# Transposing 24 token blocks by 32x32 squares and device memory instead of on TensorE, tiles through device memory too, and a later GpSimd split

## The chip, the core and the metric

The kernel runs on one core of a Trainium2 chip. The metric is the device time of one execution in microseconds (us): 2503.42 us before, the median of 3 runs from 2503.2 to 2503.71. Engines are named by the profile's letters: PE is TensorE's matmul, PEld its weight load, DVE is VectorE, ACT ScalarE, POOL GpSimd, SP SyncE. ACTq is ScalarE's own queue, where it issues its transfers.

## What is computed

One transformer layer between two half-weighted feed-forward blocks, on 4 x 1024 tokens of 512 values, all in float32:

```python
def ffn(x, W1, W2, W3):                       # W1, W3 (2048, 512), W2 (512, 2048)
    hidden = silu(x @ W1.T) * (x @ W3.T)
    return fwht(hidden) @ W2.T                # Walsh-Hadamard transform over the 2048
def attn(x, wq, wk, wv, wo, inv_freq):
    q, k = rope(heads(x @ wq.T)), rope(heads(x @ wk.T)); v = heads(x @ wv.T)   # 16 heads of 32
    weights = softmax(einsum("bshd,bstd->bsht", q, k) / sqrt(32))   # heads of one token among themselves
    return einsum("bsht,bstd->bshd", weights, v).reshape(b, s, 512) @ wo.T
x = x + 0.5 * ffn(layernorm(x), W1, W2, W3)
x = x + attn(layernorm(x), wq, wk, wv, wo, inv_freq)
x = x + 0.5 * ffn(layernorm(x), W1, W2, W3)
```

The scores are taken between the 16 heads of each token, so attention needs nothing from other tokens.

## The kernel before

The 4096 tokens are 8 tiles of 512, and a tile is 4 blocks ("subs", numbered 0 to 31) of 128 tokens. There are 16 passes, numbered 0 to 15: each of the 8 tiles runs through the feed-forward twice, and `PASSES` holds the order, `(1, t)` for a tile's first time and `(2, t)` for its second. The Walsh-Hadamard transform is folded into W2 during pass 0. Every float32 matrix product is made of three fp32r matmuls, with both operands split into a high and a low part (L608 to L610, `products`; for the down projection also L639, L640 and L643).

**A pass.** `feed_forward(p)` has 16 steps n of 128 hidden values. In a step TensorE makes the gate and the up half, 2 x 4 x 3 = 24 matmuls of 512 columns from the tile's transposed input `xt` (`up`), and then adds the hidden slice of the step before to the 4 banks of `acc`, 4 x 3 = 12 matmuls (`down`). ScalarE applies SiLU (L1076), VectorE multiplies by the up half (L1584), ScalarE copies the product to fp32r (L1084, the high part), VectorE subtracts (L1591, the low part). TensorE needs both parts of step n-1 only after it has made up(n). At the end of a pass there is no next up step: down(14) follows up(15) at once, and down(15) waits for L1591 of step 15.

**Attention** is done by VectorE between these steps, for blocks whose q, k and v are ready. It is cut in 512 units, 16 a block, each a product and a reduction of 128 x 1024 (L1311 and L1323 for scores, L1316 and L1325 for values). `UNITS_TO` says how many units a pass does, and `units_by_step` deals them out over its steps, against planned costs: 2.5 for a unit, and a cost of its own for each piece of other VectorE work (`beside`) in a step. ScalarE's exponential of a block stands ahead of or behind its hidden copy of a step (`EXP_AHEAD`, `EXP_BEHIND`), which follows from where the units stand.

**Gaps.** Between two passes TensorE makes q, k and v of two or three new blocks (`new_subs(p)`), 12 matmuls for each of q, k and v of a block, and in some passes the output projection of a tile. Passes 5, 14 and 15 (`LATE`) take a tile through attention's output projection right before its second feed-forward: their gap is `late_gap`, all others' is `early_gap`. A block is "early" when its tile was finished a pass ahead; 24 of the 32 are. `rope(g)` rotates q and k of block g on VectorE (four products L1281 from PSUM, four sums L1293 and L1294 from SBUF), and TensorE's first up step of a pass waits for the rotation of the second new block (`s_rope`), as it needs its PSUM banks.

**Who transposes what.** A matmul needs the token axis across columns, so a normalised block must be transposed. For an early block VectorE normalises it in step 13 (`Q_APPLY`, L1225) into `prod[:, 2]`; TensorE transposes it with four 128 x 128 matmuls against the identity (`transpose_sub`, L689), which stand between up(15) and down(14) of the pass ahead of an `early_gap`, and inside a `late_gap`; ScalarE and VectorE split the result from PSUM to `sub_xt` (L935, L1189). The tile of the next pass, where that is not `LATE` (11 passes, `MOVED`), goes another way: VectorE normalises it in steps 8 and 9 and transposes it within 32 x 32 squares (L1562), 16 transfers of 64 KB from SBUF to SBUF (`move`, L945, four in each of steps 10 to 13) put the squares in place, ScalarE copies the high part in step 14 (L952), and VectorE subtracts in step 15 (L1568). Finished attention outputs of five tiles go through device memory in squares as well (`keep_output` L957, `move_outputs` L966).

**The first gap.** After pass 0 GpSimd still splits the four raw attention weights (L1164). The last four of these splits, for the output projection, run beside `rope(0)`. ScalarE may write the values of the first blocks only when they are done (`s_wattn` 4).

**Weights.** SyncE loads 1 MB of up weights (L573) and 512 KB of down weights (L576) for every step from device memory, two buffers each.

## Time and profile before

| | |
|---|---|
| median of 3 runs | 2503.42 us |
| the profiled execution | 2501.66 us |
| its span | 2499.8 us, granted clock 1.0 |
| PE busy | 2489.7 us, 100% of the span, 11111 instructions |
| DVE busy | 2044.3 us, 82%, 2602 |
| ACT busy | 530.2 us, 21%, 796 |
| POOL busy | 63.0 us, 3%, 109 |
| DMA | 459.48 MB; SyncE's queue 46.0% and ScalarE's 5.7% of the 16 engines |
| device memory | 408.04 MB read, 38.80 MB written |

The chain of work that ended last is 90% PE and 8% DVE. The share of a busy engine counts from the start of its first to the end of its last overlapping instruction: a matmul of 512 columns is listed with 0.39 us, but they follow each other every 0.227 us. In a timeline row stand the start, the duration, engine, line, operation, written and read tiles with their shapes, the count of merged instructions, and in brackets the idle time before it and what ended it.

### The profile page before, as it was taken

Reading aid. Unit: us, or ns where it says so; the run is one execution under the profiler, and the core shown is the slowest. Engines: PE = TensorE matmul, PEld = TensorE weight load, DVE = VectorE, ACT = ScalarE, POOL = GpSimd, SP = SyncE. Lnnn points to the kernel's source line nnn. Section 1 sums busy time; section 2 is a strip of 40 time slices with the busy share of each in tenths; the row PEclk is TensorE's granted clock in tenths of the full one; section 3 lists DMA queues with packets and bytes.
Section 4 is the critical chain, followed back from the end, with each engine's and each line's share of the span. In section 5 each row is a group of like instructions: output and inputs, shape, how many; then the busy total and the mean of one; then the engine's idle time right before and its main releaser. Section 6 shows DMA issues by size and latency. Waiting matters only on the chain.

```text
span 2499.8 us, 30169 instructions
## 1 busy us (share of the span) xinstructions
PE 2489.7 (100%) x11111; PEld 2061.4 (82%) x11111; DVE 2044.3 (82%) x2602; ACT 530.2 (21%) x796; POOL 63.0 (3%) x109
## 2 busy tenths in 40 slices
PE   9999999999999999999999999999999999999999
PEld 7878888888888888888888888888888888888887
DVE  9569989699786997979969899797986979878711
ACT  3332212222121221222212122122121212211211
POOL 0030000000000000000000000000000000000000
PEclk9999999999999999999999999999999999999999
DMA  9645635455352564645635466454562545535364
GB/s 343 254 188 181 218 145 200 131 202 210 135 201 81 210 216 162 224 131 206 207 109 188 168 229 208 146 220 144 202 221 93 197 148 219 190 107 199 137 219 165
DMA packets 161172, 459.48 MB, mean 184 GB/s; under 512 B 53312, under 2 KB 82240, under 8 KB 127808
## 3 DMA queue, kind: packets, MB, share of 16 engines
q1 hardware_dynamic: 81792, 419.73, 46.0%
q10 hardware_dynamic: 79296, 38.68, 5.7%
q8 instruction: 46, 0.75, 0.1%
q14 instruction: 38, 0.31, 0.0%
HBM read 408.04 MB, written 38.80 MB: 179 GB/s over the span
## 4 chain that ended last, share of the span: by engine, by line
PE 90%; DVE 8%; issue 1%; DMA 0%; ACT 0%; POOL 0%; SPq 0%; DVEq 0%; ACTq 0%; POOLq 0%
PE gu L608 19%; PE gu L610 19%; PE gu L609 19%; PE acc L639 8%; PE acc L640 8%; PE acc L643 8%; PE acc L608 2%; PE acc L610 2%; PE acc L609 2%; DVE scores L1323 1%; DVE mixed L1325 1%; DVE prod L1316 1%; DVE prod L1311 1%; PE acc L736 1%; DVE gated L1584 1%
## 5 line engine op out<-in xcount | busy, mean ns | idle before, releaser
L608 PE MATMUL gu<-xt,w_up 128*128 128x512 f32 x2048 | 798.4, 390 | 0.2
L610 PE MATMUL gu<-xt,w_up 128*128 128x512 f32 x2048 | 796.8, 389 | 0.0
L609 PE MATMUL gu<-xt,w_up 128*128 128x512 f32 x2048 | 796.7, 389 | 0.0
L608 PEld LDWEIGHTS gu<-xt,w_up 128*128 128x128 f32 x2048 | 384.4, 188 | 80.7 <-issue 0.8
L609 PEld LDWEIGHTS gu<-xt,w_up 128*128 128x128 f32 x2048 | 384.4, 188 | 80.0
L610 PEld LDWEIGHTS gu<-xt,w_up 128*128 128x128 f32 x2048 | 384.4, 188 | 79.8
L1584 DVE TENSOR_TENSOR gated<-gated,gu 128x512 f32<-128x512 f32 x240 | 162.8, 679 | 239.8 <-PE gu L610 238.3
L639 PE MATMUL acc<-w_down,hid 128*128 128x512 f32 x896 | 349.6, 390 | 0.0
L640 PE MATMUL acc<-w_down,hid 128*128 128x512 f32 x896 | 348.6, 389 | 0.0
L1084 ACT ACTIVATE hid<-gated 128x512 fp32r<-128x512 f32 x240 | 152.0, 633 | 892.2 <-DVE gated L1584 882.6
L1325 DVE TENSOR_REDUCE mixed<-prod 128x64 f32<-128x1024 f32 x256 | 310.1, 1213 | 0.0
L1311 DVE TENSOR_TENSOR prod<-tok 128x1024 f32<-128x1024 f32 x256 | 309.1, 1219 | 1.0
L1323 DVE TENSOR_REDUCE scores<-prod 128x32 f32<-128x1024 f32 x256 | 309.6, 1213 | 0.0
L1316 DVE TENSOR_TENSOR prod<-scores,tok 128x1024 f32<-128x1024 f32 x256 | 307.6, 1213 | 1.2
L1076 ACT ACTIVATE gated<-gu 128x512 f32<-128x512 f32 x240 | 143.7, 599 | 591.5 <-PE gu L610 588.5
L643 PE MATMUL acc<-w_down,hid 128*128 128x512 f32 x896 | 239.5, 389 | 0.0
L643 PEld LDWEIGHTS acc<-w_down,hid 128*128 128x128 f32 x896 | 168.2, 188 | 35.0
L640 PEld LDWEIGHTS acc<-w_down,hid 128*128 128x128 f32 x896 | 168.2, 188 | 34.6
L639 PEld LDWEIGHTS acc<-w_down,hid 128*128 128x128 f32 x896 | 168.2, 188 | 34.6
L1591 DVE TENSOR_TENSOR hid<-gated,hid 128x512 fp32r<-128x512 f32 x240 | 163.8, 682 | 20.2 <-ACT hid L1084 20.2
L608 PE MATMUL gu<-w_attn,sub_xt 128*128 128x512 f32 x232 | 90.7, 391 | 0.0
L609 PE MATMUL gu<-w_attn,sub_xt 128*128 128x512 f32 x232 | 90.3, 389 | 0.0
(144 smaller groups left out, 1946.8 us busy)
## 6 DMA issues: line engine op xcount, KB each, us to landing
w_up<-up_pairs SPq DMA_DIRECT2D x240, 1024.0 KB, 4.9
w_down<-down_pairs SPq DMA_DIRECT2D x240, 512.0 KB, 3.5
up_pairs<-w_up SPq DMA_DIRECT2D x16, 1024.0 KB, 5.1
xt<-tok ACTq DMA_DIRECT2D x176, 64.0 KB, 4.1
prod<-up_raw SPq DMA_DIRECT2D x16, 512.0 KB, 6.3
down_pairs<-w_attn SPq DMA_DIRECT2D x4, 2048.0 KB, 18.4
out<-x ACTq DMA_DIRECT2D x7, 1024.0 KB, 5.3
x<-x ACTq DMA_DIRECT2D x6, 1024.0 KB, 6.5
```

The lines of the kernel that those rows point to most:

```text
L608: nc.tensor.matmul(o, w_hi, m_hi, start=first, stop=False)
L609: nc.tensor.matmul(o, w_hi, m_lo, start=False, stop=False)
L610: return nc.tensor.matmul(o, w_lo, m_hi, start=False, stop=last)
L639: nc.tensor.matmul(acc[:, s, :], h_hi[:, s * P:(s + 1) * P], hi, start=first, stop=False)
L640: nc.tensor.matmul(acc[:, s, :], h_hi[:, s * P:(s + 1) * P], lo, start=False, stop=False)
L643: ins = nc.tensor.matmul(acc[:, s, :], h_lo[:, s * P:(s + 1) * P], hi, start=False, stop=False)
L1311: return nc.vector.tensor_tensor(prod[:, buf, :].rearrange("p (h t d) -> p h t d", h=2, t=HEADS), wide(q[:, h:h + 2, None, :], 2, HEADS), ...
L1316: return nc.vector.tensor_tensor(prod[:, buf, :].rearrange("p (h d t) -> p h d t", h=2, d=HD), wide(scores[:, g % 2, h:h + 2, None, :], 2, ...
L1323: return nc.vector.tensor_reduce(scores[:, g % 2, h:h + 2, :], prod[:, buf, :].rearrange("p (h t d) -> p h t d", h=2, t=HEADS), AX.X, ALU.add)
L1325: return nc.vector.tensor_reduce(mixed[:, h:h + 2, :], prod[:, buf, :].rearrange("p (h d t) -> p h d t", h=2, d=HD), AX.X, ALU.add)
L1584: nc.vector.tensor_tensor(by_token(gated[:, u, :]), by_token(gated[:, u, :]), from_bank(gu[:, 2 * u + 1, :], p), ALU.mult).then_inc(s_h, 1)
L1591: nc.vector.tensor_tensor(low, gated[:, u, :], high.bitcast(FP32), ALU.subtract).then_inc(s_hid_lo, 1)
```

## The change

Five things are changed.

1. **Early blocks.** TensorE no longer transposes the 24 early blocks (`MOVED_SUBS`). VectorE normalises them in step 11 instead of 13 and transposes each in place within 32 x 32 squares. ScalarE stores each to device memory in step 12 (`keep_sub_squares`, 256 KB), reads it back in place in four transfers of 64 KB with pieces of 128 bytes (`move_sub`, the first block in step 13, the second in step 14), and copies the high part in step 15 (`moved_sub_high`, for all early blocks). VectorE subtracts (`moved_sub_low`). The eight blocks that are not early (0, 1, 2, 4, 11, 18, 24, 27) keep TensorE's transpose.
2. **Tiles.** A tile's squares no longer go from SBUF to SBUF. One transfer of 1 MB stores them in step 10 (`keep_squares`), four of 256 KB with pieces of 512 bytes read them back in step 11 (`move`), and the high copy stands in step 13 instead of 14.
3. **ScalarE's order.** In a step the stores and reads now come ahead of the exponentials that stand behind the hidden copy.
4. **The gap's order.** Where the second new block isn't early (blocks 4 and 24, ahead of passes 2 and 11), its transpose moves from between q and k of the first block to behind them, and v of the first block now comes before q and k of the second.
5. **GpSimd.** The last four weight splits wait for `rope(0)`.

The planner's cost of step `Q_APPLY` becomes 1.25 a block, which deals the units out a little differently: in pass 5 from `3 3 2 3 3 3 2 2 2 2 2 3 3 2 3 0` to `3 3 3 2 3 3 2 3 1 2 3 1 3 3 3 0`.

```diff
-X_STATS, X_APPLY, X_MOVE, X_SPLIT, Q_STATS, Q_APPLY = 6, 8, 10, 14, 10, 13
+X_STATS, X_APPLY, X_KEEP, X_MOVE, X_SPLIT = 6, 8, 10, 11, 13
+Q_STATS, Q_APPLY, Q_KEEP, Q_MOVE, Q_SPLIT = 10, 11, 12, 13, 15
+MOVED_SUBS = {g: at for at, g in enumerate(g for p in range(2, NP) for g in early_subs(p))}
-    beside[Q_APPLY] += 0.55 * len(early_subs(p + 1))
+    beside[Q_APPLY] += 1.25 * len(early_subs(p + 1))
+        tile_squares = nc.dram_tensor("tile_squares", [P, SUBS * D], FP32).ap()
+        sub_squares = nc.dram_tensor("sub_squares", [2, P, D], FP32).ap()
...
# TensorE
-            def query_key(g, between=None):
-                split_ready("q", g, 0)
+            def query_key(g):
+                if g in MOVED_SUBS:
+                    pe.wait_ge(s_sub_lo, MOVED_SUBS[g] + 1)
+                else:
+                    split_ready("q", g, 0)
...
             def late_gap(p):
-                output(p, 0)
-                output(p, 1)
-                if new:
-                    pe.wait_ge(s_added, SUBS * p)
-                    transpose_sub(new[0])
-                    transpose_sub(new[1])
-                output(p, 2)
-                output(p, 3)
+                for s in range(SUBS):
+                    output(p, s)
                 if new:
                     pe.wait_ge(s_x2, SUBS * i + 2)
                     query_key(new[0])
-                    split_ready("q", new[1], 0)
...
                 pe.wait_ge(s_h, HT * p)
+                query_key(new[0])
+                pe.wait_ge(s_added, SUBS * p)
                 if is_early(p, 1):
-                    query_key(new[0])
+                    query_key(new[1])
+                    value(new[0])
                 else:
-                    query_key(new[0], lambda: transpose_sub(new[1]))
-                pe.wait_ge(s_added, SUBS * p)
-                query_key(new[1])
-                value(new[0])
+                    transpose_sub(new[1])
+                    value(new[0])
+                    query_key(new[1])
...
                 else:
-                    pe.wait_ge(s_h, n0 + HT - 1)
-                    for g in early_subs(after):
-                        transpose_sub(g)
                     down_step(last, 0, False, False)
                 down_step(last, 1, False, True)
...
# ScalarE
-            def move(p, q):
-
+            def keep_squares(p):
                 act.wait_ge(s_turned, SUBS * MOVED[p] + SUBS)
-                squares = turned.rearrange("p (k f c) -> p k f c", k=KT, f=QUADS)
+                act.dma_start(tile_squares, turned).then_inc(s_squares_kept, 16)
+
+            def move(p):
+
+                act.wait_ge(s_squares_kept, 16 * MOVED[p] + 16)
+                squares = tile_squares.rearrange("(q i) (k f c) -> f i k q c", q=QUADS, k=KT, f=QUADS)
...
+            def keep_sub_squares(g):
+                act.wait_ge(s_sub_turned, MOVED_SUBS[g] + 1)
+                act.dma_start(sub_squares[new_subs(next_of(g)).index(g)], sub_normed(g)).then_inc(s_sub_kept, 16)
+
+            def move_sub(g):
+
+                later = max(early_subs(next_of(g)))
+                act.wait_ge(s_sub_kept, 16 * MOVED_SUBS[later] + 16)
+                squares = sub_squares[new_subs(next_of(g)).index(g)].rearrange("(q i) (k f j) -> f i k q j", q=QUADS, k=KT, f=QUADS)
+                for f in range(QUADS):
+                    act.dma_start(sub_split(g)[1][32 * f:32 * f + 32].bitcast(FP32).rearrange("p k (q j) -> p k q j", q=QUADS),
+                                  squares[f]).then_inc(s_sub_moved, 16)
+
+            def moved_sub_high(g):
+                later = max(early_subs(next_of(g)))
+                act.wait_ge(s_sub_moved, 16 * QUADS * (MOVED_SUBS[later] + 1))
+                high, low = sub_split(g)
+                nc.scalar.activation(high, low.bitcast(FP32), ACT.Copy).then_inc(s_sub_hi, 1)
...
                     nc.scalar.activation(hidden(u)[0], gated[:, u, :], ACT.Copy).then_inc(s_hid_hi, 1)
-                    if n == HT - 1 and after < NP and after not in LATE:
+                    for g in OUTPUT_KEEP.get((p, n), ()):
+                        keep_output(g)
+                    if after in MOVED and n == X_KEEP:
+                        keep_squares(after)
+                    if after in MOVED and n == X_MOVE:
+                        move(after)
+                    if after < NP and n == Q_KEEP:
                         for g in early_subs(after):
-                            sub_high(g)
+                            keep_sub_squares(g)
+                    if after < NP and Q_MOVE <= n < Q_MOVE + len(early_subs(after)):
+                        move_sub(early_subs(after)[n - Q_MOVE])
                     for g in EXP_BEHIND.get((p, n), ()):
                         exp(g)
-                    for g in OUTPUT_KEEP.get((p, n), ()):
-                        keep_output(g)
-                    if after in MOVED and X_MOVE <= n < X_MOVE + QUADS:
-                        move(after, n - X_MOVE)
                     if after in MOVED and n == X_SPLIT:
                         moved_high(after)
+                    if after < NP and n == Q_SPLIT:
+                        for g in early_subs(after):
+                            moved_sub_high(g)
...
# GpSimd
                 for k in range(KT):
+                    if m == O and k == 0:
+                        pool.wait_ge(s_rope, 1)
...
# VectorE
+            def moved_sub_low(g):
+                dve.wait_ge(s_sub_hi, MOVED_SUBS[g] + 1)
+                high, low = sub_split(g)
+                nc.vector.tensor_tensor(low, low.bitcast(FP32), high.bitcast(FP32), ALU.subtract).then_inc(s_sub_lo, 1)
...
                             for s, g in enumerate(early):
                                 ln_apply(key, s, sub_normed(g), x_of(g))
+                            for s, g in enumerate(early):
+                                dve.wait_ge(s_ln, ln_done(key, s))
+                                squares = sub_normed(g).rearrange("p (f j) -> p f j", j=32)
+                                nc.vector.transpose(squares, squares).then_inc(s_sub_turned, 1)
```

The order of instructions shows it at four places. First TensorE at the end of pass 3, between up(15) (`gu<-xt,w_up`) and down(14) (`acc<-w_down,hid`), before:

```order
L609 MATMUL gu<-xt,w_up 128x512
L610 MATMUL gu<-xt,w_up 128x512
L689 MATMUL gu<-ident,prod 128x128 x8
L639 MATMUL acc<-w_down,hid 128x512
L640 MATMUL acc<-w_down,hid 128x512
```

and now:

```order
L619 MATMUL gu<-xt,w_up 128x512
L620 MATMUL gu<-xt,w_up 128x512
L649 MATMUL acc<-w_down,hid 128x512
L650 MATMUL acc<-w_down,hid 128x512
L649 MATMUL acc<-w_down,hid 128x512
```

The eight transposes are gone, and the down step follows the up step directly.

TensorE in the gap ahead of pass 2, before, where q of block 3 ends, block 4 is transposed and k of block 3 begins:

```order
L609 MATMUL gu<-w_attn,sub_xt 128x512
L610 MATMUL gu<-w_attn,sub_xt 128x512
L689 MATMUL gu<-ident,prod 128x128 x4
L608 MATMUL gu<-w_attn,sub_xt 128x512
L609 MATMUL gu<-w_attn,sub_xt 128x512
```

and now, where k of block 3 ends, block 4 is transposed and v of block 3 begins:

```order
L619 MATMUL gu<-w_attn,sub_xt 128x512
L620 MATMUL gu<-w_attn,sub_xt 128x512
L699 MATMUL gu<-ident,prod 128x128 x4
L618 MATMUL acc<-w_attn,sub_xt 128x512
L619 MATMUL acc<-w_attn,sub_xt 128x512
```

q and k of block 4 (24 matmuls) used to stand ahead of v of blocks 3 and 4, and stand now between the two.

ScalarE from the hidden copy of step 13 of pass 5 on (the next pass has blocks 12 and 13 early), before (the gate's SiLU is `gated<-gu`, the hidden copy `hid<-gated`):

```order
L1084 ACTIVATE hid<-gated 128x512
L945 DMA xt<-tok 32x4x128 x4
L1076 ACTIVATE gated<-gu 128x512
L1084 ACTIVATE hid<-gated 128x512
L957 DMA out_squares<-tok 128x512
L952 ACTIVATE xt<-xt 128x1024 x2
L1076 ACTIVATE gated<-gu 128x512
L1084 ACTIVATE hid<-gated 128x512
L935 ACTIVATE sub_xt<-gu 128x512 x2
```

and now:

```order
L1113 ACTIVATE hid<-gated 128x512
L974 DMA sub_xt<-sub_squares 32x16x32 x4
L959 ACTIVATE xt<-xt 128x1024 x2
L1105 ACTIVATE gated<-gu 128x512
L1113 ACTIVATE hid<-gated 128x512
L986 DMA out_squares<-tok 128x512
L974 DMA sub_xt<-sub_squares 32x16x32 x4
L1105 ACTIVATE gated<-gu 128x512
L1113 ACTIVATE hid<-gated 128x512
L981 ACTIVATE sub_xt<-sub_xt 128x512 x2
```

The four transfers of block 12 are followed by the tile's copy in step 13, those of block 13 stand in step 14, and the blocks' copies of step 15 read `sub_xt` where the transfers have put it, not PSUM.

VectorE in pass 5, around the normalising of blocks 12 and 13, before in step 13:

```order
L1311 TENSOR_TENSOR prod<-tok 128x1024
L1323 TENSOR_REDUCE scores<-prod 128x32
L1225 TENSOR_SCALAR prod<-x,mean_var,rstd 128x512 x2
L1584 TENSOR_TENSOR gated<-gated,gu 128x512
L1311 TENSOR_TENSOR prod<-tok 128x1024
```

and now in step 11:

```order
L1357 TENSOR_TENSOR prod<-scores,tok 128x1024
L1366 TENSOR_REDUCE mixed<-prod 128x64
L1638 TENSOR_TENSOR hid<-gated,hid 128x512
L1266 TENSOR_SCALAR prod<-x,mean_var,rstd 128x512 x2
L1625 STREAM_TRANSPOSE prod<-prod 128x512 x2
L1631 TENSOR_TENSOR gated<-gated,gu 128x512
L1357 TENSOR_TENSOR prod<-scores,tok 128x1024
```

Two transposes of 128 x 512 stand behind the two normalisations, and the next step's product waits behind them.

## Rows read from the trace of the kernel before

**Rows 1.** The page's busy times by engine: us, share, instructions.
```profile
PE 2489.7 (100%) x11111; PEld 2061.4 (82%) x11111; DVE 2044.3 (82%) x2602; ACT 530.2 (21%) x796; POOL 63.0 (3%) x109
```

**Rows 2.** TensorE's waits over the span: total us, times, longest.
```profile
PE gu L608 <- DVE tok L1294: 2.2, 1, 2.2
...
PE acc L608 <- DVE hid L1591: 0.8, 2, 0.4
PE gu L689 <- DVE prod L1225: 0.6, 2, 0.4
```

**Rows 3.** TensorE's timeline at the end of pass 2: start, us, instruction.
```profile
460.46 0.40 PE L610 MATMUL gu<-xt,w_up 128*128 128x512 f32 x1
460.70 1.04 PE L689 MATMUL gu<-ident,prod 128*128 128x128 f32 x8
...
461.81 0.40 PE L640 MATMUL acc<-w_down,hid 128*128 128x512 f32 x1
```

**Rows 4.** TensorE's timeline at the end of pass 1.
```profile
312.16 0.39 PE L610 MATMUL gu<-xt,w_up 128*128 128x512 f32 x1
312.40 0.60 PE L689 MATMUL gu<-ident,prod 128*128 128x128 f32 x4
...
313.06 0.40 PE L640 MATMUL acc<-w_down,hid 128*128 128x512 f32 x1
```

**Rows 5.** VectorE's timeline at the end of pass 1, step 15.
```profile
312.66 0.69 DVE L1584 TENSOR_TENSOR gated<-gated,gu 128x512 f32<-128x512 f32 x1
314.05 0.69 DVE L1591 TENSOR_TENSOR hid<-gated,hid 128x512 fp32r<-128x512 f32 x1 [0.70 <-ACT hid L1084]
```

**Rows 6.** Window: us, busy us (xcount) of PE, PEld, DVE, ACT, POOL; passes 3, 5, 6, 8, 9.
```profile
500.60:620.00 119.40, 119.40 (x528) 98.86 (x527) 116.10 (x136) 26.35 (x38) 2.10 (x4) 1.00 0.57 207
...
819.40:938.80 119.40, 119.40 (x528) 98.82 (x527) 118.78 (x140) 26.35 (x38) 2.10 (x4) 1.00 0.63 227
967.20:1086.60 119.40, 119.40 (x529) 98.80 (x528) 118.68 (x143) 29.09 (x41) 2.10 (x4) 1.00 0.63 225
...
1293.80:1413.20 119.40, 119.40 (x528) 98.84 (x527) 118.77 (x140) 26.36 (x38) 2.10 (x4) 1.00 0.58 209
1441.60:1561.00 119.40, 119.40 (x528) 98.81 (x527) 117.84 (x142) 29.22 (x41) 2.10 (x4) 1.00 0.64 228
```

**Rows 7.** Timelines at the end of passes 5 and 6, TensorE.
```profile
938.81 1.03 PE L689 MATMUL gu<-ident,prod 128*128 128x128 f32 x8
...
1086.58 1.03 PE L689 MATMUL gu<-ident,prod 128*128 128x128 f32 x8
```

**Rows 8.** Timelines at the end of passes 5 and 6, VectorE.
```profile
939.30 0.68 DVE L1584 TENSOR_TENSOR gated<-gated,gu 128x512 f32<-128x512 f32 x1
...
1088.54 0.68 DVE L1584 TENSOR_TENSOR gated<-gated,gu 128x512 f32<-128x512 f32 x1
```

**Rows 9.** VectorE's timeline in step 8 of pass 5.
```profile
890.48 1.30 DVE L1562 STREAM_TRANSPOSE tok<-prod 128x512 f32<-128x512 f32 x2
891.70 0.65 DVE L1584 TENSOR_TENSOR gated<-gated,gu 128x512 f32<-128x512 f32 x1
```

**Rows 10.** VectorE's timeline in the gap ahead of pass 2, rotating block 4.
```profile
330.33 0.69 DVE L1281 TENSOR_TENSOR prod<-gu,cos_t 128x512 f32<-128x512 f32 x1 [1.49 <-PE gu L610]
...
333.96 0.42 DVE L1294 TENSOR_TENSOR tok<-prod 128x256 f32<-128x256 f32 x1
```

**Rows 11.** The first gap: GpSimd's timeline.
```profile
165.68 5.38 POOL L1164 TENSOR_TENSOR w_attn<-tok,w_attn 128x512 fp32r<-128x512 f32 x4 [2.08 <-ACT w_attn L1043]
```

**Rows 12.** The first gap: VectorE's timeline.
```profile
168.44 1.50 DVE L1294 TENSOR_TENSOR tok<-prod 128x256 f32<-128x256 f32 x1
169.86 1.48 DVE L1293 TENSOR_TENSOR tok<-prod 128x256 f32<-128x256 f32 x1
```

**Rows 13.** ScalarE's transfer issues of L945: ns min/median/max.
```profile
L945 ACTq DMA_DIRECT2D xt<-tok x176: 592/622/1395, 272.6 to 2023.2; - x176
```

**Rows 14.** ScalarE's transfer issues of L966: ns min/median/max.
```profile
L966 ACTq DMA_DIRECT2D xt<-out_squares x20: 578/1650/4993, 463.5 to 1876.2; - x20
```

More of the change, by code:

```diff
@@ L173, in transposed @@
         elif p in LATE:
-            order += att + [("q", g, 0) for g in new[:2]] + [("x", p, k) for k in range(KT)]
+            order += att + [("x", p, k) for k in range(KT)]
         else:
-            order += [("q", g, 0) for g in early_subs(p)]
             order += [("q", g, 0) for j, g in enumerate(new[:2]) if not is_early(p, j)] + att
@@ L359, in build @@
         s_turned = sem("s_turned")
+        s_squares_kept = sem("s_squares_kept")
         s_moved = sem("s_moved")
@@ L362, in build @@
         s_moved_lo = sem("s_moved_lo")
+        s_sub_turned = sem("s_sub_turned")
+        s_sub_kept = sem("s_sub_kept")
+        s_sub_moved = sem("s_sub_moved")
+        s_sub_hi = sem("s_sub_hi")
+        s_sub_lo = sem("s_sub_lo")
         s_att_turned = sem("s_att_turned")
@@ L696, in project @@
                 return ins
-            def query_key(g, between=None):
-                split_ready("q", g, 0)
+            def query_key(g):
[3 more added lines that the diff above has]
+                    split_ready("q", g, 0)
                 project(Q, qk_bank(g)[:, Q, :], sub_split(g), 0)
-                if between is not None:
-                    between()
                 project(K, qk_bank(g)[:, K, :], sub_split(g), 0).then_inc(s_qk, 1)
@@ L952, in moved_high, with next_of @@
                     nc.scalar.activation(X[:, 0, ks, :], X[:, 1, ks, :].bitcast(FP32), ACT.Copy).then_inc(s_moved_hi, 1)
+            def next_of(g):
+                return next(p for p in range(2, NP) if g in new_subs(p))
+            def keep_sub_squares(g):
[13 more added lines that the diff above has]
+                nc.scalar.activation(high, low.bitcast(FP32), ACT.Copy).then_inc(s_sub_hi, 1)
             def keep_output(g):
@@ L1113, in gap @@
                     attention_high(p)
-                    for g in new[:2]:
-                        sub_high(g)
                     for k in range(KT):
@@ L1576, in beside @@
                         if n == Q_APPLY:
+                            if after in MOVED:
+                                dve.wait_ge(s_turned, SUBS * MOVED[after] + SUBS)
                             for s, g in enumerate(early):
                                 ln_apply(key, s, sub_normed(g), x_of(g))
+                            for s, g in enumerate(early):
+                                dve.wait_ge(s_ln, ln_done(key, s))
+                                squares = sub_normed(g).rearrange("p (f j) -> p f j", j=32)
+                                nc.vector.transpose(squares, squares).then_inc(s_sub_turned, 1)
                 for n in range(HT):
@@ L1594, in feed_forward @@
                         for g in early:
-                            sub_low(g)
+                            moved_sub_low(g)
                     beside(n)
@@ L1615, in late_gap @@
                         for g in new[:2]:
-                            sub_low(g)
+                            moved_sub_low(g)
                 ln_means(key, at, last_of(key))
@@ L1668, in early_gap @@
                         dve.wait_ge(s_added, SUBS * (p - 1) + 1)
-                    else:
-                        dve.wait_ge(s_tp, TP["q", new[0], 0] + 1)
                     sub_stats(just[0])
```

6 lines of the change are left out of this document (3 added, 3 removed).

## The prediction

> **What bounds the kernel now.** I read the page's busy times first. TensorE is busy for 2489.7 us of a span of 2499.8, VectorE for 2044.3 [rows 1]. So nearly every microsecond taken from TensorE's stream counts, unless a wait takes its place. TensorE's waits come next: the list adds up to some 8 us, and three entries matter here: 2.2 us once behind a rotation of VectorE (L1294), 0.8 us in two waits of 0.4 at a pass's end behind the hidden low part (L1591), and 0.6 us in two waits of a transpose [rows 2]. Third, busy time by pass, because VectorE's 82% is a mean. In passes 5, 6 and 8 VectorE is busy for 118.7 to 118.8 of 119.4 us, so between two products there is no idle time; pass 9 has 0.9 us less work, and pass 3 has 2.7 us less [rows 6]. The same rows give TensorE's pitch, 119.4 us for 528 listed matmuls or 0.227 us each, so that 12 matmuls take 2.72 us and 24 take 5.44. The timelines of TensorE and VectorE at a pass's end come last, since there down(14) is the only cover for the hidden split of step 15.
>
> **TensorE's transposes.** At the end of pass 2 eight of them stand between the matmuls that start at 460.46 and 461.81. That is 1.35 us, of which two pitches (0.45) would be there anyway: 0.90 us for two blocks [rows 3]. Four of them at the end of pass 1 give 0.90 - 0.45 = 0.45 us for one block [rows 4]. The listed durations (1.04 and 0.60) overlap their neighbours and aren't used. 24 blocks x 0.447 us = **10.7 us less**. 20 of the blocks stand at pass ends and four in the two late gaps, where the output projections follow each other and VectorE follows them with the same distance as before, so I count those whole.
>
> **What is late next at a pass's end.** Without transposes TensorE arrives at down(15) 2.72 us after up(15). In pass 1 up(15) ends at 312.40 [rows 4], the product starts at 312.66, and the low part ends at 314.05 + 0.69 = 314.74 [rows 5]: 2.34 us, or 0.26 us to the product's start and 2.08 from there. That fits under 2.72 with 0.4 us to spare, so in a pass whose VectorE is on time the transposes' time is won in full. But each pass gets VectorE work. One more transpose pair: the pair L1562 starts at 890.48 and the next product at 891.70, so **1.22 us** for two blocks [rows 9]. It comes in step 11, and where there is idle time behind it, it costs nothing. Passes 5, 6 and 8 have none [rows 6]:
> - Pass 5: the last product starts 939.30 - 938.81 = 0.49 us after up(15) [rows 7, 8]. Then 0.49 + 1.22 + 2.08 = 3.79, against 2.72: a wait of 1.1 us. Pass 8 has the same busy time [rows 6], so another 1.1.
> - Pass 6: 1088.54 - 1086.58 = 1.96 [rows 7, 8]. Then 5.26 against 2.72, 2.5 us, of which one of the 0.4 us waits was there [rows 2]: 2.1 more.
> - Pass 9: its 0.9 us less busy time takes up most of the pair; about 0.3.
>
> Together **4.6 us more**. The ends of this term are 0 (the planner, whose cost for the step rises, finds room that the rows don't show) and about 9 (each of the other eight passes also gets half a microsecond, for the units come out in other steps and VectorE's lateness in a step reaches 5 us or more). I take the value by rows, since a VectorE without a gap can't hide anything. The other wait of 0.4 us, in pass 2, I leave as it is: ScalarE's tile copy moves from before the last SiLU, but VectorE's last reduction ends late there too.
>
> **The gaps ahead of passes 2 and 11.** Block 4 (and 24) is projected later: behind its q and k only v of one block stands, 2.72 us, where there were two, 5.44. The first up step needs the rotation's end. It starts about 0.2 us after the matmuls and runs from 330.33 to 333.96 + 0.42 = 334.38, so 4.05 us [rows 10]. 0.2 + 4.05 - 2.72 = 1.5 us of waiting, twice: **3.1 us more**. The bounds are 0 and 4.5 (block 3's rotation also starts later, behind the split of block 4). The transpose itself comes 2.7 us later than now and no longer waits for its normalised input: **0.6 us less** [rows 2].
>
> **The first gap.** Beside GpSimd's four splits (165.68 to 171.06) [rows 11] two sums of `rope(0)` take 1.50 and 1.48 us [rows 12], where the same instruction takes 0.42 with GpSimd idle [rows 10]. With the splits behind the rotation these 2.1 us go, and TensorE's wait of 2.2 us [rows 2] with them: **2.1 us less**. What is behind the wait: the rotation then ends at about 169.6 and the splits at 175.0; ScalarE writes its first value block after TensorE's next 24 matmuls, 16 transposes and 12 matmuls (5.4 + 1.8 + 2.7 us), at about 179.5, so nothing is held up. `rope(1)` meets the last split and may lose one microsecond; TensorE has the tile's transposes in front of it there.
>
> **Transfers and ScalarE.** A pass with a tile issued 16 transfers over four steps; now it issues 1, 4, 2, 4 and 4 in steps 10 to 14. One L945 issue takes 0.62 us [rows 13], so four take 2.5 us, as a step's four do today. From the hidden copy to the next SiLU ScalarE has 4.4 us (a step of 8.16 minus 1.0 and 2.72), and VectorE needs that SiLU only 2.7 us later. But L966's issues (2048 pieces each) take from 0.58 to 4.99 us, 1.65 in the median [rows 14]; 0.6 + 5.0 + 2 x 1.65 makes 8.9 us for four. The new transfers have 512 pieces each. So a step's issues cost between 2.5 and 8.9 us; I take 2.5 to 4.5, since 2048 pieces in all are what a single L966 has, and hidden either way. Stores land a step ahead of the reads that wait for them, and the reads of step 14 have 8 us until the copy of step 15. I cost all of this at nothing.
>
> The Trainium skill speaks against this part: DMA: Bandwidth & Descriptors (Specifications) puts the least size for full rate at 512 B, and has smaller pieces read and modified, so the blocks' 128-byte pieces would be the slow kind. In this trace the only 128-byte reads are L966's, and they are the slow ones. By the rule alone the sum would move to the fourth rival below; by the count of pieces it stays.
>
> **Sum.** -10.7 + 4.6 + 3.1 - 0.6 - 2.1 = -5.7 us. The profiled execution took 2501.66 us, which makes 2496.0 for it; it lies 1.8 us under the median of the runs, so the median goes from 2503.42 to **2497.7 us**.
>
> **Rivals.**
> 1. *VectorE's extra work is absorbed.* For it: 18% of VectorE is idle over the span, and the planner now knows the cost. Against it: passes 5, 6 and 8 are full by the rows. Then -10.7 + 3.1 - 0.6 - 2.1 = -10.3: 2493.1 us.
> 2. *VectorE's lateness spreads.* Half a microsecond at the ends of the other eight passes: 2501.7 us. For it: only 0.4 us of cover is left anywhere. Against it: those passes had 1 us and more of idle time.
> 3. *The removed time was filler everywhere*, because the splits of the blocks (which now wait for a transfer) come late: TensorE needs them 5.4 us after up(15), and they are ready at about 4. It would give no change, 2503 us.
> 4. *Slower: ScalarE's issues block.* If the four small-piece reads of step 14 take 8.9 us as L966's can, they begin 1.0 us after up(14) and end 1.7 us after up(15). The last SiLU (0.6) then ends at 2.3, and product, copy and subtraction (2.1) at 4.4: a wait of 1.7 us in nine passes and about 3 us more in the three full ones, 24 us in all. 2497.7 + 24 = 2522 us. It decides from issues of 6 us on, which is where the SiLU comes later than up(15). Short of that it gives nothing.
>
> **Numbers.** Forecast 0.50, rival 1 0.20, rival 2 0.15, rival 3 0.05, rival 4 0.07, and 0.03 for what I don't see. What a measurement can tell from no change is 0.2%, 5.0 us, so the border is 2498.4 us, right beside my number. The forecast's own range is 2494.5 to 2500.5, and I give it 0.29 faster and 0.21 same. With rival 1 that makes 0.49 faster; the forecast's 0.21 with rivals 2 and 3 makes 0.41 the same; rival 4 and the unseen make 0.10 slower. The range 2491 to 2505 takes in rivals 1 to 3 and leaves out the fourth.
>
> **What would show it.** No transpose row at the ends of passes 2 to 13, and 96 transposes fewer. TensorE's waits behind the hidden low part: 1.1 us in passes 5 and 8, 2.5 in pass 6. A wait of 1.5 us of the first up step behind the rotation in passes 2 and 11. No wait in the first gap, and sums of 0.42 us there. ScalarE's issues of `sub_xt` at 0.6 us each; a single one of over 3 us would point to rival 4. The forecast is wrong if VectorE's last product starts no later than now in pass 5, or if TensorE waits inside a pass.

## The result, and the profile after

The changed kernel takes **2515.12 us** (median of 8 runs, 2509.21 to 2522.78), against 2503.39 us for the kernel before on the same chip: a ratio of 1.0049 [1.0039, 1.0059], slower by 12 us where I forecast 6 us less. The profiled execution is the slowest of the eight, 2522.78 us with a span of 2521.0; so its waits are those of the worst of the eight, and their sum is more than the median lost. The page's busy times, to be held against [rows 1]:

```profile
PE 2488.4 (99%) x11015; PEld 2055.8 (82%) x11015; DVE 2058.8 (82%) x2626; ACT 531.1 (21%) x796; POOL 63.5 (3%) x109
```

The 96 transposes are gone (11111 to 11015), and VectorE has 14.5 us more. TensorE's waits, whose counterparts are [rows 2] (line, waited for, total us, times, longest):

```profile
PE gu L618 <- DVE sub_xt L1247: 14.6, 4, 5.1
PE acc L618 <- DVE hid L1638: 8.0, 7, 3.2
PE gu L618 <- DVE tok L1335: 4.1, 3, 1.4
```

The first line is new: four times TensorE waits for the low part of a block's input. The single waits from TensorE's timeline, in the gaps ahead of passes 1 and 2 and at the ends of passes 5, 6, 8 and 11 (a wait for `sub_xt` is that of the first product of the gap behind):

```profile
178.06 0.47 PE L618 MATMUL gu<-w_attn,xt 128*128 128x512 f32 x1 [1.20 <-DVE tok L1335]
335.27 0.50 PE L618 MATMUL gu<-xt,w_up 128*128 128x512 f32 x1 [1.43 <-DVE tok L1335]
...
941.52 0.47 PE L618 MATMUL acc<-w_down,hid 128*128 128x512 f32 x1 [2.42 <-DVE hid L1638]
948.26 0.77 PE L618 MATMUL gu<-w_attn,sub_xt 128*128 128x512 f32 x1 [3.74 <-DVE sub_xt L1247]
1098.26 0.47 PE L618 MATMUL acc<-w_down,hid 128*128 128x512 f32 x1 [3.20 <-DVE hid L1638]
1102.56 0.47 PE L618 MATMUL gu<-w_attn,sub_xt 128*128 128x512 f32 x1 [1.32 <-DVE sub_xt L1247]
1425.44 0.47 PE L618 MATMUL acc<-w_down,hid 128*128 128x512 f32 x1 [1.13 <-DVE hid L1638]
1432.87 0.77 PE L618 MATMUL gu<-w_attn,sub_xt 128*128 128x512 f32 x1 [4.43 <-DVE sub_xt L1247]
1895.99 0.77 PE L618 MATMUL gu<-w_attn,sub_xt 128*128 128x512 f32 x1 [5.13 <-DVE sub_xt L1247]
```

Read the end of pass 5 on ScalarE and VectorE. The reads of the second block (L974) are issued at 932.27, behind an output's store:

```profile
931.90 0.33 ACTq L986 DMA_DIRECT2D out_squares<-tok  x1
932.27 6.30 ACTq L974 DMA_DIRECT2D sub_xt<-sub_squares  x4
938.67 0.60 ACT L1105 ACTIVATE gated<-gu 128x512 f32<-128x512 f32 x1 [6.14 <-issue]
939.30 0.69 DVE L1631 TENSOR_TENSOR gated<-gated,gu 128x512 f32<-128x512 f32 x1 [1.18 <-ACT gated L1105]
940.02 0.63 ACT L1113 ACTIVATE hid<-gated 128x512 fp32r<-128x512 f32 x1 [0.75 <-DVE gated L1631]
946.76 1.15 ACT L981 ACTIVATE sub_xt<-sub_xt 128x512 fp32r<-128x512 f32 x2 [6.12 <-DMA sub_xt<-sub_squares]
```

The same four issues by themselves (ns of one, least, median and longest, with the first and last start; then us from an issue to its landing):

```profile
L974 ACTq DMA_DIRECT2D sub_xt<-sub_squares x4: 564/772/4101, 932.3 to 937.9; - x4
DMA to landing us min/median/max: 6.4/9.2/9.7
```

Two things went wrong. The four issues took 6.30 us instead of 2.6, one of them 4.10 us by itself, so the SiLU behind them started at 938.67 and VectorE's last product waited 1.18 us for it. And ScalarE's copy, ready after 940.65, waited 6.12 us for the data, which landed 14 us after the first issue; VectorE's subtraction and TensorE's q follow it. The window view of these microseconds (us, busy us of the engines, then granted clock, DMA share, GB/s) shows the DMA engines full while TensorE waits (SyncE's loads of the up and down weights are issued at 931.8 and 931.0, and again at 936.7 and 939.3), and TensorE's clock at half behind the wait:

```profile
936.00:941.00 5.00, 3.10 (x14) 2.25 (x12) 3.13 (x4) 1.23 (x2) 0.00 (x0) 1.00 1.02 324
941.00:947.00 6.00, 3.00 (x12) 2.17 (x12) 0.37 (x1) 0.24 (x1) 0.00 (x0) 0.96 0.61 165
948.00:950.00 2.00, 1.74 (x4) 1.48 (x5) 2.00 (x4) 0.00 (x0) 0.00 (x0) 0.50 0.00 0
950.00:952.00 2.00, 2.00 (x6) 1.52 (x6) 2.00 (x3) 0.00 (x0) 0.00 (x0) 0.50 0.00 0
952.00:954.00 2.00, 2.00 (x8) 1.58 (x7) 1.38 (x3) 0.00 (x0) 0.00 (x0) 0.66 0.00 0
```

The four passes have one thing in common: where the second block's reads fall against SyncE's up loads. In passes 5, 8 and 11 they are issued 0.50, 0.48 and 0.33 us behind one and in pass 6 2.18 us behind one, and the four issues take 6.30, 3.72, 4.28 and 3.21 us. In the other seven passes that read a second block they come 1.1 to 2.7 us ahead of an up load and take 2.6 to 2.8 us, as in pass 3:

```profile
613.55 2.80 ACTq L974 DMA_DIRECT2D sub_xt<-sub_squares  x4
614.61 5.23 SPq L583 DMA_DIRECT2D w_up<-up_pairs  x2
```

Back at the end of pass 5, from 948.26 on twelve matmuls take until 953.44, 5.2 us instead of 2.7. Behind the wait of 4.43 us twelve take 5.2 us too, and behind that of 5.13 us seven take 3.0 instead of 1.6: 6.4 us for the three places. The account of the span: it grew by 21.2 us, which is -10.7 for the transposes, +23.1 of waits (26.7 in the three lines above, 3.6 in [rows 2]) and 8.8 left. The clock's 6.4 is the part of them that rows show; 2.4 us stay open.

### The profile page after: what moved, and what is told of

Same layout as the page of the kernel before. It is cut to its first block, busy times and chain, and to the rows that moved or that the text cites. A ratio compares the mean times of both kernels' runs of the same rounds, so it can differ in the third digit from the quotient of the medians.

```text
span 2521.0 us, 29999 instructions
## 1 busy us (share of the span) xinstructions
PE 2488.4 (99%) x11015; PEld 2055.8 (82%) x11015; DVE 2058.8 (82%) x2626; ACT 531.1 (21%) x796; POOL 63.5 (3%) x109
## 4 chain that ended last, share of the span: by engine, by line
PE 72%; DVE 21%; issue 3%; DMA 2%; ACTq 1%; ACT 0%; POOL 0%; DVEq 0%; SPq 0%; POOLq 0%
PE gu L618 16%; PE gu L619 15%; PE gu L620 15%; PE acc L650 6%; PE acc L653 6%; PE acc L649 6%; DVE mixed L1366 4%; DVE scores L1364 4%; DVE prod L1357 3%; DVE prod L1352 3%; PE acc L618 2%; PE acc L620 2%; PE acc L619 2%; DVE gated L1631 2%; DMA sub_xt<-sub_squares 2%
## 5 line engine op out<-in xcount | busy, mean ns | idle before, releaser
L618 PE MATMUL gu<-w_attn,sub_xt 128*128 128x512 f32 x232 | 93.4, 403 | 14.6 <-DVE sub_xt L1247 14.6
L619 PE MATMUL gu<-w_attn,sub_xt 128*128 128x512 f32 x232 | 92.7, 400 | 0.0
```

Source lines behind the costliest of these rows:

```text
L618: nc.tensor.matmul(o, w_hi, m_hi, start=first, stop=False)
L619: nc.tensor.matmul(o, w_hi, m_lo, start=False, stop=False)
```

## The experiments

Every kernel's ratio is against the kernel before on the same chip, whose median was 2501.9 to 2503.4 us in the four sets.

**1. The chain of the blocks one step earlier.**

```diff
-Q_STATS, Q_APPLY, Q_KEEP, Q_MOVE, Q_SPLIT = 10, 11, 12, 13, 15
+Q_STATS, Q_APPLY, Q_KEEP, Q_MOVE, Q_SPLIT = 9, 10, 11, 12, 15
```

> The blocks' statistics, products, stores and reads are each issued one step earlier (steps 9, 10, 11, 12 and 13 in place of 10 to 14); the low part is still made at step 15. Theory A (late landing): the changed kernel lost its time because the second block's four reads, issued in step 14, landed 10.7 to 14.1 us later in passes 5, 6, 8 and 11, and TensorE waited 14.6 us for what is made of them and then ran at half the clock. One step is some 9 us, so the waits for the blocks' low part at the ends of those passes fall from 14.6 us to under 2 and the clock loss of some 9 us goes with them: about 2515 - 13 - 8 = 2494 to 2500. Theory B (VectorE is late by its own work, 1.2 us per transposed pair): its work is the same, so the ends of the full passes wait as before: 2512 to 2518. Theory C (the tiles' transfers and the order of the exponentials cost it): untouched, 2512 to 2518.

Measured: 2533.79 us, 1.0125 [1.0108, 1.0142]. None of the theories. No wait for the blocks' low part is left, so the late landing is cured as theory A had it, but now the blocks' store stands in step 11 behind the tile's reads. ScalarE's timeline in pass 3:

```profile
598.16 4.40 ACTq L952 DMA_DIRECT2D xt<-tile_squares  x4
602.60 2.32 ACTq L966 DMA_DIRECT2D sub_squares<-prod  x2
605.02 0.60 ACT L1105 ACTIVATE gated<-gu 128x512 f32<-128x512 f32 x1 [6.66 <-issue]
606.38 0.63 ACT L1113 ACTIVATE hid<-gated 128x512 fp32r<-128x512 f32 x1 [0.75 <-DVE gated L1631]
613.98 2.64 ACTq L974 DMA_DIRECT2D sub_xt<-sub_squares  x4
616.72 0.60 ACT L1105 ACTIVATE gated<-gu 128x512 f32<-128x512 f32 x1 [9.71 <-issue]
```

The reads wait from 607.0 to 613.98 for the store to land, and the SiLU that is queued behind them and their issues starts after 9.71 us without work on ScalarE. TensorE then waits for the hidden low part, the second line of the changed kernel's list:

```profile
PE acc L618 <- DVE hid L1638: 24.4, 9, 4.2
```

This kernel changed two things at once, the steps and the order against the tile's reads, so it doesn't test the theories' prices. What it shows is that here the reads' wait in front of their issue, which holds up ScalarE's queue, costs more (31 us over the kernel before) than the late landing that it cures (the changed kernel lies 12 us over it).

**2. Exponentials ahead of the transfers within a step.**

```diff
                     nc.scalar.activation(hidden(u)[0], ...).then_inc(s_hid_hi, 1)
+                    for g in EXP_BEHIND.get((p, n), ()):
+                        exp(g)
                     for g in OUTPUT_KEEP.get((p, n), ()):
...
-                    for g in EXP_BEHIND.get((p, n), ()):
-                        exp(g)
```

> Within a step ScalarE issues the exponentials ahead of the stores and reads, as in the kernel before; everything else as in the changed kernel. Theory A (late landing of the block reads in four passes): only pass 11 got its late reads through an exponential that stood behind the tile's reads, so its 5.1 us wait and some 2 us of clock go: about 2507 to 2511. Theory C (the order of exponentials is the cause): the waits go in all four passes, 2495 to 2500. Theory B (VectorE's own work): 2512 to 2518.

Measured: 2519.78 us, 1.0066 [1.0049, 1.0083], which overlaps the changed kernel's interval. The long wait of pass 11 is gone from the trace, as A had it (those of passes 5 and 8 are left, 3.64 and 4.25 us), but a wait of 3.24 us for the hidden low part came in pass 2 and one of 4.27 in pass 6 (3.20 and 1.32, in two waits, in the changed kernel). So the order of the exponentials (theory C) is not the cause, and A's gain of 4 to 8 us did not come: in the trace it was given back in passes 2 and 6, and the time lies above the range of every theory.

**3 and 4. Tiles alone, blocks alone.** The first is the kernel before with the tile's store, reads and split in steps 10, 11 and 13 and GpSimd's wait; the second is the changed kernel with

```diff
-                    if after in MOVED and n == X_MOVE:
-                        move(after)
+                    if after in MOVED and X_MOVE <= n < X_MOVE + QUADS:
+                        move(after, n - X_MOVE)
```

and the old sixteen transfers from `turned` in `move`.

> The kernel before, with the token tiles' squares stored to and read from device memory and GpSimd's last split behind the rotation, and nothing else: the blocks keep TensorE's transposes and the exponentials their place. Theory A (the block reads are the cause): no long wait, within 3 us of the kernel before, 2500 to 2506. Theory C (the tiles' transfers are the cause): most of the loss stays, 2510 to 2520.

> The changed kernel, with the token tiles moved by the sixteen transfers within on-chip memory of the kernel before (steps 10 to 13, copy at step 14). Theory A: the block reads of step 14 stay, so the loss stays: 2511 to 2520, with waits of 3 to 5 us for the blocks' low part at the ends of the full passes. Theory C (the tiles' transfers): 2495 to 2503. If the sixteen transfers' issue on ScalarE costs more than the tile's five, the time is above 2520.

Measured: tiles alone 2500.04 us (2499.73 to 2500.65), 0.9989 [0.9980, 0.9999]; blocks alone 2518.93, 1.0065 [1.0048, 1.0082]. The loss is in the blocks. The first kernel gains 3.1 us by the medians, of which experiment 7 finds 1.0 for GpSimd's wait; its interval nearly reaches no change. In the second kernel the waits are divided otherwise than A said, 14.1 us for the hidden low part and 3.0 for the blocks'. I read the two as one chain on ScalarE, in which a microsecond or two decides which of them catches TensorE; no run tests this.

**5, 6 and 10. The reads in larger pieces, a short transpose, and both.** These lighten the reads and VectorE's work one at a time and then together.

```diff
-                squares = sub_squares[...].rearrange("(q i) (k f j) -> f i k q j", q=QUADS, k=KT, f=QUADS)
+                rows = sub_squares[...].rearrange("p (k c) -> p k c", k=KT)
                 for f in range(QUADS):
-                    act.dma_start(....rearrange("p k (q j) -> p k q j", q=QUADS), squares[f]).then_inc(s_sub_moved, 16)
+                    act.dma_start(..., rows[32 * f:32 * f + 32]).then_inc(s_sub_moved, 16)
```

```diff
-                                squares = sub_normed(g).rearrange("p (f j) -> p f j", j=32)
+                                squares = sub_normed(g)[:, :32].rearrange("p (f j) -> p f j", j=32)
```

> The changed kernel, but each of a block's four reads fetches 32 rows of four 512-byte pieces (512 pieces a block) in place of 2048 pieces of 128 bytes; the same bytes, issues and waits. It leaves out the rearranging of the squares, so the projections get wrong values. Theory A1 (the pieces' number makes the reads land late beside the weights' loads): the reads issue in under 2.7 us and land within 6 us, the waits for the blocks' low part (14.6 us) and the half clock behind them go: 2495 to 2503. Theory B (VectorE comes late by its own added work, whatever the reads cost): 2510 to 2518. Theory A2 (it is the store and the wait for its landing on ScalarE, not the pieces): 2510 to 2518, with the reads' issue short all the same.

> The changed kernel, but VectorE turns only the first 32 of a block's 512 columns (a transpose of some 0.1 us in place of 0.6); it leaves out the rest of the turning, so the projections get wrong values. Stores, reads and order stay. Theory A1 (number of pieces): the loss stays but for VectorE's 1 us a pass: 2507 to 2515. Theory B (VectorE's added 1.2 us a pass makes everything behind it late): the waits of passes 5, 6, 8 and 11 go: 2493 to 2500.

> The changed kernel with both lightenings, 512-byte pieces and a transpose of 32 columns; it leaves out most of the turning, so the projections get wrong values. Theory A (two conditions make the loss: VectorE's added 1.2 us brings the reads beside the weights' loads, and their 2048 pieces make them long there): each alone gave back most, both together give back the rest: 2493 to 2499, with no wait over 2 us but those of the rotation. If they gave back the same microseconds twice and a third cause stays (the short waits for the hidden low part), 2500 to 2504.

Measured: 2505.83 us (2501.65 to 2512.39), 1.0014 [1.0005, 1.0024]; 2502.28 us (2500.51 to 2513.04), 1.0008 [0.9997, 1.0019]; both 2499.18 us (2496.40 to 2505.45), 0.9984 [0.9975, 0.9994]. From the changed kernel's 1.0049 that is 0.35%, 0.41% and 0.65%: 9, 10 and 16 us. Neither A1 nor B alone is right: each edit gives back most of the 12 us, both together more than either and less than the sum of 19. In pass 5 the issue of the four reads, where it took 6.30 us, is in experiments 5 and 6:

```profile
932.77 1.93 ACTq L974 DMA_DIRECT2D sub_xt<-sub_squares  x4
```

```profile
931.77 3.32 ACTq L974 DMA_DIRECT2D sub_xt<-sub_squares  x4
```

The large pieces issue in 1.93 us (over all 96 issues the median of one is 0.44 us instead of 0.66), but ScalarE's copy still waits till 942.98 for them, 10 us after the first issue, where A1 had 6. What the short transpose does can be read from the loads: in passes 5, 8 and 11 the second block's reads now come 0.5 to 0.8 us ahead of the up load instead of 0.3 to 0.5 behind, and the four issues take 3.32, 2.83 and 2.69 us. In all three kernels pass 6 keeps a wait for the hidden low part (3.19, 4.27 and 4.22 us), so that one is not of the reads' length. With both light, one wait of 4.22 us for the hidden low part is left, in pass 6, where an exponential stands behind the first block's reads, and its sum on VectorE waits 2.29 us for it. So the expectation of no wait over 2 us failed, and the time lies between its two ranges.

**7. GpSimd's wait alone.** The kernel before with `pool.wait_ge(s_rope, 1)` ahead of the last split.

> The kernel before with one edit: GpSimd's last split waits for the first rotation. The first gap's wait of 2.2 us goes; in the changed kernel another of 1.2 us stands behind the second rotation, so 1.0 us is won, not the 2.1 that I predicted: 2502.4 (2501.5 to 2503). If the 3.1 us that the tiles' kernel gained are all of this edit, 2500.3.

Measured: 2500.85 us (2500.47 to 2502.26), 0.9993 [0.9984, 1.0002]: 1.0 us in the median, within the interval's reach of nothing. In its trace the rotation's sums take 0.42 us, and the four normalizations of the next tile, beside which the splits now run, take 4.84 us:

```profile
170.81 4.84 DVE L1227 TENSOR_SCALAR tok<-x,mean_var,rstd 128x512 f32<-128x512 f32 x4
```

In the kernel before the same four take 1.91 us there. The cost has moved to them and comes out as 1.2 us of waiting behind `rope(1)`. The median lies below the expected range, but so does that of the kernel before in this set (2501.86 us); the 1.0 us is as expected.

**8. The old order in the gap.** `transpose_sub(new[1])` between the first block's q and k again.

> The changed kernel, with the order of the gap before: the late block's transposes stand between the first block's query and key products. The two waits for the rotation in passes 2 and 11 (1.43 and 1.42 us) go, or become those of the transposes (0.8 us in the kernel before): 2512.5 by the trace (2511 to 2514). If the order mattered for the waits of the low part too, below 2508.

Measured: 2519.1 us (four runs, 2507.65 to 2523.82), 1.0073 [1.0057, 1.0088]. The two rotation waits went (4.1 to 1.2 us) and 1.5 us of transposes' waits came, but the time is undecided: what the edit is worth is far below the spread of 16 us. The profiled execution is its fastest. In pass 5 the reads are issued as in the changed kernel, 0.5 us behind an up load's issue and 1.3 behind a down load's, and yet

```profile
931.84 3.37 ACTq L974 DMA_DIRECT2D sub_xt<-sub_squares  x4
```

and the longest of the four took 6.2 us from issue to landing, against 9.7: the copy could start 7.8 us after the first issue instead of 14.5. The same reads at the same distance from the loads get their data several microseconds sooner or later. In pass 8 of this execution they were slow again, 4.27 us to issue and a wait of 4.67 us of TensorE.

**9 and 12. Which passes carry it.** Two kernels with both routes, on the old gap order: `BY_TENSOR = (6, 7, 9, 12)` leaves the blocks of these four passes to TensorE (16 of 24 by memory), and `BY_TENSOR = (2, 3, 4, 8, 10, 11, 13)` is the counterpart (12 of 24 by memory: the four passes and the late ones).

```diff
+BY_TENSOR = (6, 7, 9, 12)
...
+                    if after in BY_TENSOR:
+                        pe.wait_ge(s_h, n0 + HT - 1)
+                        for g in early_subs(after):
+                            transpose_sub(g)
                     down_step(last, 0, False, False)
```

> The changed kernel with the old gap order, in which the blocks of passes 6, 7, 9 and 12 (8 of 24) are turned by TensorE as in the kernel before and the other 16 by VectorE and device memory. In the changed kernel's trace only the passes ahead of these four lost time behind a late read. Theory A (the loss lies in those four collisions): 16 x 0.447 = 7.2 us of transposes are won, some 1 us more with GpSimd's split, and 1 to 3 us of short waits are lost: 2494 to 2499. Theory D (the collision moves to the passes left, since a pass that is late shifts the weights' loads against the reads anywhere): waits of over 2 us appear in passes 2, 3, 4, 7, 9, 10, 12 or 13: above 2501.

> The counterpart of the mixed kernel: only the blocks of passes 6, 7, 9 and 12, and of the late passes 5 and 14 (12 of 24), go by VectorE and device memory; TensorE turns the other 12. Old gap order. Theory A (the four collisions carry the loss by themselves): from the tiles' kernel at 2500.0, 12 x 0.447 = 5.4 us of transposes won, and the waits of passes 5, 6, 8 and 11 with their half clock lost (some 14.6 + 7.8 + 8.8 by the changed kernel's trace, less in the executions where fewer of the reads collide): 2508 to 2520, and spread over 5 us or more between executions. Theory D (the loss is the sum of small disturbances of all passes, and the four were late because the ones before were): 2495 to 2503, with a spread under 3 us.

Measured: the mixed kernel **2496.02 us** (11 runs, 2494.74 to 2500.63), 0.9973 [0.9964, 0.9982], faster than both kernels; the counterpart 2522.02 us (2519.91 to 2526.28), 1.0079 [1.0065, 1.0092]. So the four passes carry the loss by themselves, and theory D falls. The counterpart lies 2 us above theory A's range; it gives back 5.4 us of transposes, which from the changed kernel's 2515.1 makes 2520.5. In its trace the second reads of passes 5, 8 and 11 stand 0.2 to 0.5 us behind an up load again and take 5.50, 4.89 and 4.21 us to issue. The mixed kernel's waits besides 1.9 us in the prologue:

```profile
PE gu L704 <- DVE prod L1278: 1.5, 2, 0.8
PE gu L623 <- DVE tok L1347: 1.2, 1, 1.2
PE acc L623 <- DVE hid L1654: 0.9, 2, 0.5
```

and the line of all its block reads (ns of one, least, median, longest), followed by that of the counterpart:

```profile
L983 ACTq DMA_DIRECT2D sub_xt<-sub_squares x64: 564/657/760, 297.2 to 2173.2; - x64
```

```profile
L983 ACTq DMA_DIRECT2D sub_xt<-sub_squares x48: 564/657/3180, 751.1 to 2200.2; - x48
```

In the mixed kernel every second block's reads come 1.1 to 2.7 us ahead of an up load, and 64 issues of 128-byte pieces take no more than 0.76 us each.

**11. VectorE's extra work alone.** The tiles-only kernel, with the blocks normalized at step 11 and

```diff
+                                half = sub_normed(g)[:, :D // 2].rearrange("p (f j) -> p f j", j=32)
+                                chain.mark(nc.vector.transpose(half, half))
+                                dve.wait_ge(s_dve, chain.k)
+                                chain.mark(nc.vector.transpose(half, half))
```

> The kernel with only the tiles by device memory (2500.0 us), whose blocks TensorE still turns; VectorE normalizes them at step 11 in place of 13 and turns half of each twice there, which gives the same values and costs it about the changed kernel's 1.2 us a pass (some 1.3). No block store, no block read. Theory A (lateness alone costs only the short waits for the hidden low part): those of passes 5, 6, 8, 9 as I predicted, 4.6 us: 2502 to 2506. Theory B (VectorE's added work is the loss by itself): 2512 to 2520.

Measured: 2505.42 us (2503.92 to 2505.95), 1.0008 [0.9999, 1.0018], 5.4 us above the tiles' kernel in experiment 3 and spread over 2 us only. In its trace TensorE waits for the hidden low part 0.67, 2.73 and 0.69 us in passes 5, 6 and 8. The lateness by itself is small and steady; a spread of 9 us and more is seen only in kernels that read the blocks back.

## Why the prediction was wrong

**The step that failed** is the last of the change: "I cost all of this at nothing". For the tiles it holds (experiment 3). For the blocks, the step-14 reads cost in the profiled execution 14.6 us of waits for the low part, 6.4 us at half clock behind three of these, and 1.3 us more of the hidden low part's wait in pass 5 (2.42, where I had 1.1): 22 us, where the median lies 17 us above my forecast. I put the reads' cost in their issue alone, from [rows 13, 14], and took "8 us until the copy of step 15" as enough for the landing, although no row of before shows a landing beside a full DMA queue. The issue took 6.30, 3.21, 3.72 and 4.28 us in the four passes, and only in pass 5 did that reach TensorE by more than 0.3 us; the landing, 11 to 14 us after the first issue, was late in all four. One of my signs was there: a single issue of over 3 us, the 4.10 us in pass 5.

**The coupling that I did not see** is that two terms act together. VectorE's 1.22 us, which I had added as a wait of its own, also moves ScalarE's issue of the reads: in pass 5 the hidden copy ahead of them comes 4.3 us ahead of up(15)'s end, where it came 5.6 ahead in the kernel before. In passes 5, 8 and 11 the issue then falls behind an up load; without most of the transpose it is ahead of it (experiment 6). In pass 6 it is behind one either way. Experiment 11 has the lateness without reads (+5.4 us), experiment 9 the reads where lateness is absent (64 issues, no wait for a block's low part), 6 the reads with most of the lateness taken away (-10 us), and 12 both together (+22 us over the tiles' kernel despite 5.4 us of transposes won). Pass 11 was not on my list of full passes: there an exponential stood behind the tile's reads, VectorE waited 4.30 us for it, and with the exponentials ahead (experiment 2) the wait is gone.

**Rival 4** (2522 us, chance 0.07) had the right place, the reads of step 14, but not the cause: that the issue makes the SiLU and with it TensorE late is seen in pass 5 alone, not in nine passes. That its 2522 us is the profiled execution's time is luck; the median is 2515.12. The pieces, which I let their count decide, mattered: with 512 pieces of 512 bytes in place of 2048 of 128 a block, experiment 5 gives back 9 us. No run tells their size from their number.

**The other terms.**
- Transposes, -10.7: the 96 are gone. The mixed kernel, with 16 blocks' worth (7.2 us) and 1.4 us more of waits for transposes and the hidden low part, has a span 4.7 us below the tiles' kernel's, 1.1 short of their balance.
- Waits for the hidden low part, +4.6: passes 8 and 9 came as worked out (1.13 and 0.33 us). Experiment 5, whose reads issue in about 2 us, has 1.15, 3.19, 1.14 and 0.31 us in passes 5, 6, 8 and 9, where I had 1.1, 2.5, 1.1 and 0.3. So the growth of pass 5 is the reads', and pass 6 was sized 0.7 us too low for another reason. Experiment 11 has 4.1 us of them in the trace and +5.4 in the median.
- Rotations in the gaps, +3.1: 1.43 and 1.42 us, where I had 1.5 each. Right.
- First gap, -2.1: mis-sized. The wait of 2.2 us went and one of 1.20 came; 1.0 us remains. I had named `rope(1)` and thought TensorE covered; what the splits now slow are the four normalizations ahead of it (1.91 to 4.84 us).
- Transposes in the gaps, -0.6: no such wait is left. Right.
- TensorE's waits before add up to 6.6 us by the list, not to some 8; no term hangs on it.

With 1.0 in place of 2.1 and the reads at nothing the sum would have been -4.6 us. The experiments do not settle why the same reads land under 8 us after their issue in one execution and 14 in another, nor what keeps a wait of 3.2 us and more in pass 6 when both edits are light. That the waits are what halves the clock is read from their order in time, not tested apart, and it does not follow each of them: behind the 3.20 us in pass 6 the granted clock stayed at 1.00.

## What to carry to other kernels

A transfer off the critical path has two costs, the time in which it blocks the engine that issues it and the time to its landing; each needs a row that was taken beside the traffic that will be there. When one edit makes an engine later and another puts a transfer behind that engine, price them together, at the passes without idle time. A route that fails in the full stages can pay in the others: switched per stage, the kernel went from 12 us of loss to 7 us of gain, of which about 3 are the tiles' route and GpSimd's wait (experiment 3) and 4 the blocks'.

## What the runs showed of the hardware

- Four issues of 128-byte-piece reads from device memory took 2.6 us as a rule. Issued 0.2 to 0.5 us behind a 1 MB load on SyncE's queue they took 3.37 to 6.30 us (the changed kernel, experiments 8 and 12), 1.1 to 2.7 us ahead of one 2.6 to 2.9. The same bytes in 512-byte pieces took 1.7 us, and 1.7 to 1.9 about 0.5 us behind a load (experiment 5).
- Behind waits of 3.74 to 5.13 us TensorE's granted clock was 0.50 for 3 to 5 us, the lower of its two levels (1.2 GHz), and 1.00 again behind that; behind a wait of 3.20 us it stayed at 1.00, behind one of 3.24 us in experiment 2 it was 0.53.
- Four GpSimd splits (5.4 to 5.8 us) slow some VectorE instructions beside them and not others: sums of two SBUF operands from 0.42 to 1.50 us before [rows 10, 12], normalizations from 0.54 to 1.21 after, but the rotation's products, which read one operand from PSUM, took 0.68 us beside the splits in both kernels, as they do elsewhere.
